# Attention block: natural scores from 32-row tiles of the array instead of a masked key tile

## The reference

```
q = split_heads(layernorm(x) @ Wq.T + bq);  k, v = split_heads(ctx @ Wk.T + bk), split_heads(ctx @ Wv.T + bv)
scores = q k^T / sqrt(8);  scores = where(mask, finfo.min, scores)
attn = softmax(scores) v;  x = x + tanh(g_xattn) * (attn @ Wo.T + bo)
y = layernorm(x);  gate = softmax(y @ Wg + bg);  thr = sigmoid(y @ Wt + bt) / 8
w = max(gate - thr, 0), normed;  x = x + tanh(g_ffn) * sum_e w_e * (gelu(y @ W1_e + b1_e) @ W2_e + b2_e)
```

## Time and profile before

| | |
|---|---|
| median of 3 runs | 677.84 us (677.28 to 678.39) |
| the profiled execution | 676.37 us, its span 674.4 us |
| PE, busy share of the span | 94% |
| PEld | 72% |
| DVE | 81% |
| ACT | 64% |
| POOL | 28% |

### The profile page before, as it was taken

The page is one execution under the profiler, slowest core; times in us unless marked ns, Lnnn a source line. Parts: engine busy times, 40 slices in busy tenths (PEclk is TensorE's granted clock), DMA queues, the critical chain, the costliest instruction groups (busy, mean ns, idle before and its releaser), DMA issues.

```text
span 674.4 us, 14486 instructions
## 1 busy us (share of the span) xinstructions
PE 635.5 (94%) x3964; PEld 483.3 (72%) x3964; DVE 544.5 (81%) x1085; ACT 433.8 (64%) x764; POOL 185.6 (28%) x240
## 2 busy tenths in 40 slices
PE   3999999999999999739999999999999999999998
PEld 2666666766666666427878878878788788787886
DVE  5778888998898888545888888888888888888886
ACT  3466666666666666417766766767667667666673
POOL 6224444444444442200121221221212212212121
PEclk9999999999999999958999999999999999999999
DMA  6544344444444444103112112111111111121110
GB/s 190 141 121 123 106 119 120 117 113 114 118 114 113 113 106 106 58 0 71 48 48 63 47 48 64 47 47 62 47 49 60 47 62 47 47 62 47 46 63 17
DMA packets 37402, 52.74 MB, mean 78 GB/s; under 512 B 9344, under 2 KB 20480, under 8 KB 37376
## 3 DMA queue, kind: packets, MB, share of 16 engines
q1 hardware_dynamic: 37376, 52.42, 28.4%
HBM read 26.58 MB, written 2.23 MB: 43 GB/s over the span
## 4 chain that ended last, share of the span: by engine, by line
PE 85%; DVE 6%; DMA 3%; SPq 2%; issue 2%; ACT 2%; POOL 0%; DVEq 0%; ACTq 0%; POOLq 0%
PE ps_h L1081 9%; PE ps_y L1061 9%; PE ps_y L1063 9%; PE ps_y L1062 9%; PE ps_h L1083 9%; PE ps_h L1082 9%; PE scores L1014 5%; PE scores L1015 4%; PE scores L1022 3%; PE scores L1023 3%; DVE neg_max L659 3%; PE heads L1033 3%; PE misc L902 2%; PE misc L903 2%; PE misc L904 2%; PE misc L888 2%
## 5 line engine op out<-in xcount | busy, mean ns | idle before, releaser
L632 ACT ACTIVATE h_sb<-ps_h,b_sb 128x512 f32<-128x512 f32 x256 | 175.9, 688 | 109.2 <-PE ps_h L1083 95.7
L846 DVE TENSOR_TENSOR h_low<-h_sb,h_high 128x512 fp32r<-128x512 f32 x256 | 164.4, 682 | 0.0
L842 DVE CAST h_high<-h_sb 128x512 fp32r<-128x512 f32 x128 | 98.8, 772 | 67.9 <-ACT h_sb L632 67.9
L528 POOL TENSOR_TENSOR yT<-yT,weighted 128x512 f32<-128x512 f32 x54 | 69.8, 1293 | 300.9 <-DVE weighted L834 300.9
L1081 PE MATMUL ps_h<-x_high,w_high 128*128 (+1 forms) x256 | 103.1, 403 | 1.7 <-ACT h_sb L632 1.6
L1061 PE MATMUL ps_y<-h_high,w_high 128*128 128x512 f32 x256 | 101.4, 396 | 0.8 <-DVE h_low L846 0.8
L1063 PE MATMUL ps_y<-h_high,w_low 128*128 128x512 f32 x256 | 101.3, 396 | 0.0
L1062 PE MATMUL ps_y<-h_low,w_high 128*128 128x512 f32 x256 | 101.2, 395 | 0.0
L1083 PE MATMUL ps_h<-x_high,w_low 128*128 (+1 forms) x256 | 100.6, 393 | 0.0
L1082 PE MATMUL ps_h<-x_low,w_high 128*128 (+1 forms) x256 | 100.2, 391 | 0.0
L659 DVE TENSOR_REDUCE neg_max<-scores 128x4 f32<-128x512 f32 x128 | 83.6, 686 | 9.8 <-PE scores L1023 9.2
(11 more groups left out here) (128 smaller groups left out, 1000.9 us busy)
## 6 DMA issues: line engine op xcount, KB each, us to landing
w_row<-w_scratch SPq DMA_DIRECT2D x64, 256.0 KB, 3.1
k_masked<-k_stack SPq DMA_DIRECT2D x64, 128.0 KB, 2.4
k_cur<-k_stack SPq DMA_DIRECT2D x16, 512.0 KB, 3.0
q_masked<-q_stack SPq DMA_DIRECT2D x64, 96.0 KB
w_raw<-in_w_ffn SPq DMA_DIRECT2D x16, 256.0 KB, 2.7
ctx_sb<-in_ctx SPq DMA_DIRECT2D x16, 128.0 KB, 2.1
out_y<-y_out SPq DMA_DIRECT2D x7, 256.0 KB, 2.3
probs<-in_wqk SPq DMA_DIRECT2D x2, 256.0 KB, 3.1
```

The source lines that it names most:

```text
L632: nc.scalar.activation(h_sb[:, j % HBUF, :], ps_h[:, j % 4, :], ACT.Gelu_apprx_tanh, bias=b1_sb[:, j:j + 1]).then_inc(h_done, 1)
L842: V.tensor_copy(h_high[:, j % HBUF, :], h_sb[:, j % HBUF, :]).then_inc(high_odd, 1)
L846: V.tensor_tensor(h_low[:, j % HBUF, :], h_sb[:, j % HBUF, :], h_high[:, j % HBUF, :].bitcast(F32), ALU.subtract).then_inc(low2_done, 1)
```

## The change

`natural` no longer takes one slab (4 heads, one matmul over 128 rows) but one block of 32 rows in both u = 0 and u = 1: head block r + u of every slab. For each of 4 slabs and each of two row blocks it issues a matmul of 32 rows x 128 columns of weights (from `q_stack`) with 128 moving columns straight from `k_stack`. Block u goes to bank 2 + u, and each bank gets its mask matmul of 512 columns at the end. One call thus fills both banks, and waits for both to be read. Calls go from 8 to 4 in a trip: natural(0,0), natural(0,2), natural(1,0), natural(1,2). Two of them stay in the places of the first of their pair, one takes the place of slab 3 of sequence 0 (after the turn of x2T). `k_masked`, its zeroing on POOL and its four DMAs with their waits go.

```
-                    for r in range(ROWS):
-                        rows = slice(32 * r, 32 * r + 32)
-                        sp.dma_start(k_masked[rows, r, :, :].bitcast(F32), k_stack[rows, :, :].bitcast(F32)).then_inc(km_in, 16)
...
-            nc.gpsimd.memset(k_masked[:].bitcast(F32), 0.0).then_inc(pad_done, 1)
...
-            def max_slab(group, b, s):
-                dve.wait_ge(scoresN_full[s % 2], fill_of(group, b, s))
-                nc.vector.tensor_reduce(neg_max[:, b, :, s],
-                                        scores[:, 2 + s % 2, :].rearrange("p (r k) -> p r k", k=S),
-                                        AX.X, ALU.max, negate=True).then_inc(scoresN_read[s % 2], 1)
+            def max_block(group, b, r):
+                dve.wait_ge(scoresN_full[r % 2], fill_of(group, b, r))
+                nc.vector.tensor_reduce(neg_max[:, b, r, :],
+                                        scores[:, 2 + r % 2, :].rearrange("p (s k) -> p s k", k=S),
+                                        AX.X, ALU.max, negate=True).then_inc(scoresN_read[r % 2], 1)
...
-                        wait_count(dve, km_in, g * (ROWS * 16))
+                        wait_count(dve, scoresN_full[1], fill_of(g - 1, GB - 1, ROWS - 1))
...
-                    pe.wait_ge(km_in, g * (ROWS * 16) + ROWS * 16)
+                    misc_wait_read(pe, "p01", it - 1)
+                    misc_wait_read(pe, "p23", it - 1)
                     misc_wait_read(pe, "p45", it)
                     misc_wait_read(pe, "p67", it)
                     pe.wait_ge(masknxt_done, g + 1)
                     natural(g, 0, 0)
-                    natural(g, 0, 1)
                 if (g := group_at(it, 0)) is not None:
                     transposed(g, 1, 2)
                     transposed(g, 1, 3)
-                if (g := group_at(it, 1)) is not None:
-                    natural(g, 0, 2)
                 if (g := group_at(it, -1)) is not None:
                     pe.wait_ge(x2n_done, g * GB + GB)
                     turn("x2T", lambda b: x2n[:, b, :])
                 if (g := group_at(it, 1)) is not None:
-                    natural(g, 0, 3)
+                    natural(g, 0, 2)
...
-            def natural(nxt, b, s):
-
-                wait_count(pe, scoresN_read[s % 2], fill_of(nxt, b, s) - 1)
-                dst = scores[:, 2 + s % 2, :].rearrange("p (r k) -> p r k", r=ROWS)
-                mm(dst, q_stack[:, s, b * S:(b + 1) * S], k_masked[:, :, s, b * S:(b + 1) * S], start=True, stop=False)
-                mm(dst, masked_ident[:], mask_nxt[:, b, :].unsqueeze(1).to_broadcast([P, ROWS, S]),
-                   start=False, stop=True).then_inc(scoresN_full[s % 2], 1)
+            def natural(nxt, b, r):
+
+                wait_count(pe, scoresN_read[0], fill_of(nxt, b, r) - 1)
+                wait_count(pe, scoresN_read[1], fill_of(nxt, b, r) - 1)
+                for s in range(SLABS):
+                    for u in range(2):
+                        rows = slice(32 * (r + u), 32 * (r + u) + 32)
+                        mm(scores[:, 2 + u, s * S:(s + 1) * S], q_stack[rows, s, b * S:(b + 1) * S], k_stack[rows, s, b * S:(b + 1) * S],
+                           start=(s == 0), stop=False)
+                for u in range(2):
+                    dst = scores[:, 2 + u, :].rearrange("p (s k) -> p s k", s=SLABS)
+                    mm(dst, masked_ident[:], mask_nxt[:, b, :].unsqueeze(1).to_broadcast([P, SLABS, S]),
+                       start=False, stop=True).then_inc(scoresN_full[u], 1)
```

More of the change, by code:

```diff
@@ L120, in sa @@
             return sb(name, shape, dt, phase_a)
-        k_masked = sa("k_masked", [P, ROWS, SLABS, GT], F32R)
         q_masked = sa("q_masked", [P, ROWS, SLABS, GT], F32R)
@@ L236, in gated_block @@
         headsT_done = sem("headsT_done")
-        km_in = sem("km_in")
         kcur_in = sem("kcur_in")
@@ L389, in body @@
                     settle(sp)
-                    if not (isinstance(g, int) and g == 0):
+                    if isinstance(g, int) and g == 0:
+                        sp.wait_ge(pad_done, 1)
+                    else:
                         sp.wait_ge(scoresT_full[1], fill_of(g - 1, GB - 1, SLABS - 1))
@@ L738, in body @@
                 if (g := group_at(it, 1)) is not None:
-                    for s in range(SLABS):
-                        max_slab(g, 0, s)
+                    for r in range(ROWS):
+                        max_block(g, 0, r)
                     max_split(g, 0)
@@ L753, in body @@
                     ins.then_inc(misc_read[bank_of("v")], 1)
-                    max_slab(g, 1, 0)
-                    max_slab(g, 1, 1)
+                    max_block(g, 1, 0)
+                    max_block(g, 1, 1)
                 if (g := group_at(it, 0)) is not None:
@@ L764, in body @@
                 if (g := group_at(it, 1)) is not None:
-                    max_slab(g, 1, 2)
-                    max_slab(g, 1, 3)
+                    max_block(g, 1, 2)
+                    max_block(g, 1, 3)
                     max_split(g, 1)
@@ L960, in body @@
                     nc.tensor.transpose(misc[0:2 * H, bank_of("max0"), 0:S], max_parts[:, 0, :].bitcast(F32), ident[:]).then_inc(misc_full[bank_of("max0")], 1)
-                    natural(g, 1, 1)
                 if (g := group_at(it, 0)) is not None:
@@ L977, in body @@
                     natural(g, 1, 2)
-                    natural(g, 1, 3)
                 if (g := group_at(it, 0)) is not None:
```

## The result

The changed kernel takes 692.19 us (median of 4 runs, 691.68 to 692.65) against 677.56 for the kernel before (4 runs, 676.52 to 678.39): ratio 1.0231, 95% interval 1.0212 to 1.0251. The forecast was 694, slower.

The account below looks back on a forecast made before the run. PE bounds the trip, DVE close behind. Four calls at +0.30, less 0.32, plus 0.17 of stalls: +1.02 us a trip, +16.3 over 16; 676.37 + 16.3 = 692.7, median 1.5 above, so 694; range 671 to 721.

Parts of the forecast that it names:

- PE sets the trip: Attention phase: PE, busy 16.1 of some 16.4 us, bounds each trip, with DVE close behind at 14.7.
- Loads of two blocks overlap, 0.11 a step: Small matmuls of a new call: loads in two row blocks overlap, 4 steps at 0.11, so 0.44 us.
- Switching drains the array, both ways: Each new call: entering small tiles costs 0.18 to 0.20 us, leaving 0.16; call 1.22 against 0.92, +0.30.
- Both banks must be read: A natural call waits until DVE has read both banks: 0.17 us of stalls a trip.
- From there to the next trip PE's list is the same: Behind the last natural call, natural(1,2): PE's work unchanged until the next trip, DVE done before L998, no further delay.
- L960's wait goes, -0.32: Transposition of the maxima no longer waits 0.43 us for DVE, giving back 0.32 us a trip.
- Sixteen trips alike: Whole attention phase: each trip 1.02 us longer, times 16, +16.3 us.
- The copies and the zeroing are worth nothing: Removing k_masked's DMAs and POOL zeroing: 0 taken; bounds 0.1 us a trip and at most 1 us.
- one load at a time: Small loads do not overlap: 720 us with switching cost, chance 0.27; 703 with free switching, chance 0.13.
- free switching: Tile changes cost nothing: 703 us without load overlap, chance 0.13; 685 with overlap, chance 0.13.
- The cheap small tile: Small matmuls at 0.026 us with free switching, call 0.67: 665 us; chance 0.14 including neighbours half as good.

Follow-up runs that it names:

- e9: Kernel before the change, maxima taken over keys 64 to 127 only: 676.85 us, ratio 1.0001.
- e10: Kernel before the change, natural(0,2) moved between transposed(1,2) and transposed(1,3): 686.47 us, ratio 1.0144.
- e1: Changed kernel, all eight small matmuls of a call using the same block of 32 rows: 718.93 us, ratio 1.0641.
- e3: Kernel before the change, one 32-row matmul of 128 moving columns added to each natural call, 128 in all: 712.70 us, ratio 1.0533.
- e4: Kernel before the change, one full-height (128-row) matmul of 128 moving columns added to each natural call, 128 in all: 681.43 us, ratio 1.0069.
- e2: Changed kernel, the eight small matmuls of a call contracting over all 128 rows, so no small tiles: 709.94 us, ratio 1.0514.
- e7: Changed kernel, nine 256-column filler matmuls behind natural(0,0) and nine behind natural(0,2), first trip only: 689.74 us, ratio 1.0191.
- e5: Changed kernel with the four copies of the key stack to the masked tile and their waits put back: 694.37 us, ratio 1.0289.
- the repeat: Changed kernel run once more, unaltered, as the measure for the runs beside it: 691.92 us, ratio 1.0239.

## Why the prediction was right

1. *PE sets the trip.* Half right. The earlier trace rows showed 16.1 of 16.43 busy and I took the rest for small change. e9 and e10 show a second path, the copies of queries, keys and maxima behind transposed(1,3), that is some 0.3 us longer than PE's work beside it. While it holds the trip, a saving on PE between transposed(1,3) and transposed(0,0) buys nothing. In the changed kernel PE's work there is longer than the copies: from the issue of the key copy to the load are 4.3 us, and the last recorded piece of the maxima's copy stands 0.5 to 0.7 us before the load, so some 0.4 us are spare.
2. *Loads of two blocks overlap, 0.11 a step.* Right: shown by the traces and e1. On the load alone, the Trainium skill's page "TensorE: Matmul & The Clock Gate" (LDWEIGHTS) has 32 rows as dear as 128; the trace agrees, 0.18 us against 0.19, in steps of 0.11 either way. What the overlap hides is the second block.
3. *Switching drains the array, both ways.* Right in kind, too dear in size: 0.36 forecast, 0.28 measured (e3 less e4). A call that does not wait for DVE is 1.13, not 1.22, and +0.21 over the pair, not +0.30. Its small part was forecast at 0.60 and took 0.59. Leaving was the mis-sized half: 0.09, not 0.16. I had taken 0.04 off the 0.20 behind `values` for the bf16 load; why it is 0.11 less, no run shows. The rule of the Trainium skill's page "TensorEngine Tiling (Array Packing)", Key Properties, that changing the mode drains the engine, agrees with these 0.28 us for row tiles too.
4. *Both banks must be read.* I had 0.17 of stalls a trip. PE idles 0.24 us ahead of natural(1,0), the chain has 0.11 of issue ahead of natural(0,2), and three calls are 0.07 longer because their first load waits for DVE: 0.56 in all. I did not see one more: DVE writes the stacks later, and project(4), at 173.09, takes 0.34 instead of 0.12. "From there to the next trip PE's list is the same" is where my walk stopped too early. The trace of the full-height run (e2), which has longer calls still, names the wait:

```profile
163.78 0.19 PEld L887 LDWEIGHTS misc<-inT_high,wqk_high 128*128 128x128 f32 x1 [0.15 <-DVE k_stack L671]
```

   Half the maxima took 0.72 off the trip.
5. *L960's wait goes, -0.32.* It went. In the kernel before its removal alone would have been worth nothing (e9), since the copies hold that trip; in the changed kernel it makes room for a longer call.
6. *Not foreseen, in favour:* transposed(0,0) no longer stands waiting for the copies. Its chain row is 0.33, where the kernel before has 0.17 and 0.47:

```profile
161.29 0.17 issue
161.46 0.47 PE scores L1014
```

The two trips of the chains side by side, from the end of L1015 (L996) of transposed(1,1), 152.37 and 161.69, to the same point one trip on (us):

| stretch, up to the end of | before | after | |
|---|---|---|---|
| first natural call (two slabs) | 0.92 | 1.13 | +0.21, the call |
| second call (slabs 2 and 3 of sequence 0) | 2.07 | 2.46 | +0.39, the call 0.21, DVE's banks 0.07 and 0.11 |
| L960 (L943) and natural of sequence 1 | 2.55 | 2.57 | +0.02, the call 0.21 and DVE's banks 0.31, against L960's wait and a switch that L1022 already paid behind `values` (0.20) |
| last natural call | 2.07 | 2.34 | +0.27, the call 0.21 and DVE's banks 0.07 |
| transposed(0,0), L1014 (L995) | 1.96 | 1.64 | -0.32, no wait for the copies |
| next transposed(1,1) | 6.84 | 7.06 | +0.22, project(4) waits for the stacks |

Together +0.79 for this pair, +0.84 on the mean of nine. Against my terms: the four calls +0.84 where I had 1.20, the waits for DVE +0.56 where I had 0.17, L960 -0.31 as forecast. Three terms I did not have: -0.20 (natural(1,0) stands behind `values`, where the kernel before pays for leaving the column tiles), -0.31 (the copies) and +0.22 (the stacks). My own terms also add up to 1.05, not the 1.02 that I wrote. That the trip came out near 1.02 is in good part luck: errors of 0.2 to 0.4 with both signs.

7. *Sixteen trips alike.* Wrong in a small way that helped the total: the trips give 0.84 x 16 = 13.4 of the 16.5 us of span. At the first `values` the changed kernel is 3.9 us behind (39.00 against 35.12), more than its share, and behind that its clock was at half; e7 gives back 1.5 us at group 1, 0.8 for good. What the rest of the 3 us outside the trips is stays open. So a trip too dear by 0.18, 2.9 us in 16, and a start that I had priced at nothing nearly cancelled. That is luck: the total was hit better than its parts.
8. *The copies and the zeroing are worth nothing.* The zeroing was not tested. For the copies no trace shows a gain; e5 leaves up to 3 us open.

Rivals: one load at a time (720, 703) is refuted by the loads in the trace and by e1, and free switching by e3 and e4. The cheap small tile (665) is refuted by the 0.11 us from pair to pair.

## What to carry to other kernels

Count the weight loads, not only the columns. Here, with 128 moving columns a load, the load sets the step: eight small matmuls in two row blocks side by side take 0.59 us, where two masked ones of 512 columns took 0.46, and every change between full and small tiles costs about 0.28 us there and back. So fewer and longer runs of small tiles should be cheaper; no run here tried that, nor more columns a load. Before crediting a removed wait, look for a second path beside it (here a chain of DMA issues on one queue) and change one thing on it: a busy share of 98% does not say that it is alone. Where a wait has several causes, compare the landing of the one that the profile names with the start of what waited: here a rest of 0.8 us meant that another came last. A merged step that needs two buffers at once must be priced in the first trip too, where nothing else keeps TensorE busy.

## What the runs showed that I had not expected

- The maxima's speed does not matter at all in the kernel before (1.0001), and takes 0.72 us off each trip of the changed one.
- PE was busy for 1.37 of the two us from 18 and 1.20 of those from 20, idled 1.26 us ahead of 22.77, and the granted clock went from 2.4 to 1.2 GHz at about 22 us (24 in the repeat) and came back between 34 and 36. With nine matmuls in each of the two gaps the column has 1.00 in every stretch from 20 to 38 us.
- A matmul of 128 columns between two of 512 adds 0.06 to the chain at full height and 0.34 as a 32-row tile.
- With half the maxima the changed kernel reaches the copies too: in its steady trips the last recorded piece of the maxima's copy stands 0.06 us before the load of transposed(0,0), always the same. So the 0.72 is what DVE's speed is worth until the copies hold the trip; the two kernels then stand at 16.48 and 16.34 us.
